# Scaling all three quarters of the gathered rows on ACT in a graph kernel on one Trainium2 core

## The reference

```python
h = jnp.maximum(_layernorm(x, axis=-1), 0.0)
feat_all = jnp.einsum('ni,rhid->rnhd', inputs, conv_weights)      # inputs = h, 8 relations, 4 heads of 64
feat_src_e = feat_all[edge_type, edge_src]                         # a gather per edge, 256 values
el = jnp.sum(feat_src_e * attn_l[edge_type], axis=-1)
er = jnp.sum(feat_dst_e * attn_r[edge_type], axis=-1)
e = jax.nn.leaky_relu(el + er, negative_slope=LEAKY_SLOPE)
m = jax.ops.segment_max(e, edge_dst, num_segments=N_NODES)
ex = jnp.exp(e - m[edge_dst])
alpha = ex / denom[edge_dst]                                       # denom = segment_sum(ex)
h = jax.ops.segment_sum(alpha[..., None] * feat_src_e, edge_dst, num_segments=N_NODES)
...
x = x + h                                                          # then layernorm, relu and the mean network
```

## Time and profile before

| | |
|---|---|
| median of 3 runs | 2599.94 us |
| lowest, highest | 2577.82, 2600.36 us |
| profiled execution: its own time | 2594.63 us |
| profiled execution: span | 2592.7 us |
| mean granted TensorE clock | 0.884 of full |
| gather phase, first to last L1122 | 647.0 to 1450.8 us |

### The profile page before, as it was taken

How to read it: one execution, slowest core, us unless ns; L and a number is a source line. 1 busy time by engine, 2 the same in 40 slices (tenths; PEclk the granted TensorE clock), 3 DMA queues, 4 the chain that set the end, 5 groups by cost and what they waited for, 6 DMA issues and landing times. The chain is left out here.

```text
span 2592.7 us, 29932 instructions
## 1 busy us (share of the span) xinstructions
PE 2173.1 (84%) x9258; PEld 1197.8 (46%) x9259; DVE 1387.6 (54%) x3828; ACT 718.1 (28%) x2133; POOL 584.9 (23%) x549
## 2 busy tenths in 40 slices
PE   2389999995777786778776749999989999999999
PEld 1243334333555464556554424444544444544445
DVE  5779999994456564555565528878821111101001
ACT  0134444442445453445444521010000001000000
POOL 3200000004776665757575100000000000000000
PEclk7589999997776787877777879999989999999999
DMA  5024444445444443535353323222222222233432
GB/s 148 15 97 147 154 148 154 157 154 173 125 126 129 124 140 99 150 103 156 109 152 109 69 89 102 92 82 82 71 83 90 82 86 87 82 115 98 124 98 81
DMA packets 249540, 290.31 MB, mean 112 GB/s; under 512 B 53330, under 2 KB 212247, under 8 KB 249111
## 3 DMA queue, kind: packets, MB, share of 16 engines
q1 hardware_dynamic: 195278, 181.12, 22.8%
q0 software_dynamic: 24192, 67.12, 9.9%
q10 hardware_dynamic: 29896, 39.99, 4.4%
HBM read 201.20 MB, written 86.96 MB: 111 GB/s over the span
## 5 line engine op out<-in xcount | busy, mean ns | idle before, releaser
L1905 PE MATMUL PS<-a_sb,y_sb 128*128 128x512 f16 (+2 forms) x4320 | 874.3, 363 | 43.5 <-DVE y_sb L1981 30.9
L1070 POOL DMA_INDIRECT work<-feat_tab,fidx_i x504 | 543.9, 1079 | 791.3 <-issue 653.1
L1905 PEld LDWEIGHTS PS<-a_sb,y_sb 128*128 128x128 bf16 (+1 forms) x4320 | 407.9, 98 | 509.7 <-issue 69.7
L1275 PE MATMUL PS<-work,stg 128*128 128x260 f32 x1008 | 328.4, 483 | 3.2 <-issue 2.4
L1130 ACT ACTIVATE work<-work 128x64 f32<-128x64 f32 x1344 | 327.3, 332 | 7.5 <-issue 7.1
L233 DVE TENSOR_SCALAR side<-iota_c,col_t 128x512 f16<-128x512 f16 x940 | 329.0, 350 | 0.2
L243 PE MATMUL PS<-side 128*128 128x512 f16 x940 | 254.2, 383 | 20.2 <-DVE side L233 12.4
L1275 PEld LDWEIGHTS PS<-work,stg 128*128 128x128 f32 x1008 | 231.7, 242 | 71.1 <-issue 24.6
L1995 DVE TENSOR_TENSOR mean<-PS,rdeg 128x1024 f32<-128x1024 f32 (+1 forms) x24 | 27.2, 1134 | 416.0 <-PE PS L1905 415.7
L1847 ACT ACTIVATE hT<-mean,bh_c 128x512 f32<-128x512 f32 (+1 forms) x48 | 30.3, 678 | 789.4 <-DVE mean L1999 789.4
L232 DVE TENSOR_SCALAR side<-iota_c,rel 128x128 f16<-128x128 f16 x940 | 236.4, 251 | 0.2 <-PE PS L243 0.2
(11 more groups left out here) (243 smaller groups left out, 1637.0 us busy)
## 6 DMA issues: line engine op xcount, KB each, us to landing
a_sb<-a_tab SPq DMA_DIRECT2D x126, 640.0 KB, 4.3
feat_tab<-stg ACTq DMA_DIRECT2D x120, 260.0 KB, 2.1
a_tab<-side SPq DMA_DIRECT2D x235, 128.0 KB, 1.7
stg<-dst_tab SPq DMA_DIRECT2D x42, 384.0 KB
work<-feat_tab,fidx_i POOLq DMA_INDIRECT x504
h_tab<-outs SPq DMA_DIRECT2D x42, 130.0 KB
h_tab<-outs SPq DMA_DIRECT2D x8, 520.0 KB, 3.2
stg<-h_tab SPq DMA_DIRECT2D x8, 520.0 KB
```

Of the source, the lines that this page charges most:

```text
L1070: pool.indirect_dma_start(out=ring[:, s, 0:FE], out_offset=None, in_=feat_tab[:, :], in_offset=bass.IndirectOffsetOnAxis(ap=idx, axis=0)). ...
L1275: mm = pe.matmul(PS[:, OUTS[j], 0:EXT], onehot[:, t, :], ring[:, j * U + t, 0:EXT], start=(t == 0), stop=(t == U - 1), skip_group_check=True)
L1905: mm = pe.matmul(SUMS(ug, n)[:, f, :], y_sb[l % 2][0:rows_of, kb, s, f * P:(f + 1) * P], a_sb[0:rows_of, load % SLOTS, kb % KB, 0:n], star ...
```

## The change

DVE's `scale` is taken out. ACT's `scale` does a whole quarter at once and is called for all three: quarter 0 right after the weights, then `keep`, then quarter 1, and in the next step quarter 2. The semaphore `s_sd` goes; `quarter_sum` waits for `s_sa` with every quarter, now counted three to a step. At the start of the phase ACT scales quarters 0 and 1 of the first step.

```diff
@@ ACT @@
-                def scale(i, j, q, half):
-                    for u in range(half * QT // 2, (half + 1) * QT // 2):
+                def scale(i, j, q):
+                    for u in range(QT):
                         s = j * U + q * QT + u
                         for h in range(H):
                             a = ring[:, s, h * D:(h + 1) * D]
                             ins = act.activation(a, a, ACT.Copy, scale=ring[:, s, F + h:F + h + 1])
-                    if half:
-                        ins.then_inc(s_sa, 1)
+                    ins.then_inc(s_sa, 1)
...
                 def step(i, j, last=False):
                     nxt = after(i, j, 1)
-                    for half in range(2):
-                        scale(i, j, 2, half)
+                    scale(i, j, 2)
...
                     if not last:
                         act.wait_ge(s_rs, num(i, j, 2, 2))
                         weigh(*nxt)
+                        act.wait_ge(s_ex, num(*nxt, 1, 2))
+                        scale(*nxt, 0)
                     keep(i, j)
                     if not last:
-                        act.wait_ge(s_ex, num(*nxt, 1, 2))
-                        for half in range(2):
-                            scale(*nxt, 1, half)
+                        scale(*nxt, 1)
@@ PE @@
                 def quarter_sum(i, j, q):
                     pe.wait_ge(s_oh, num(i, j, NQT, q + 1))
-                    if q:
-                        pe.wait_ge(s_sa, num(i, j, NQT - 1, q))
-                    else:
-                        pe.wait_ge(s_sd, num(i, j, 1, 1))
+                    pe.wait_ge(s_sa, num(i, j, NQT, q + 1))
@@ DVE @@
-                def scale(i, j):
-                    dve.wait_ge(s_ex, num(i, j, 1, 2))
-                    tiles = slice(j * U, j * U + QT)
-                    rows = ring[:, tiles, 0:F].rearrange("p u (h d) -> p u h d", h=H)
-                    dve.tensor_tensor(rows, rows, ring[:, tiles, F:FE].unsqueeze(3).to_broadcast([P, QT, H, D]), ALU.mult
-                                      ).then_inc(s_sd, 1)
```

More of the change, by code:

```diff
@@ L992, in gnn_kernel @@
         s_fs = [nc.alloc_semaphore(f"feat_stored{i}") for i in range(2)]
-        (s_ix, s_gat, s_sa, s_sd, s_oh, s_db, s_ew, s_oT, s_er, s_sel, s_mk, s_c1, s_v, s_c2, s_r, s_c3, s_cd, s_c4,
+        (s_ix, s_gat, s_sa, s_oh, s_db, s_ew, s_oT, s_er, s_sel, s_mk, s_c1, s_v, s_c2, s_r, s_c3, s_cd, s_c4,
          s_bk, s_ex, s_fx, s_rs, s_grp, s_ev, s_hs, s_kc, s_kp, s_dc) = [sem(a) for a in (
-             "idx_ready", "quarter_summed", "quarters_scaled", "first_quarter_scaled", "onehots_ready", "dst_loaded",
+             "idx_ready", "quarter_summed", "quarters_scaled", "onehots_ready", "dst_loaded",
              "er_window_loaded", "onehotT_ready", "er_ready", "er_selected", "masks_loaded", "scores_ready",
@@ L1196, in begin @@
                     act.wait_ge(s_ex, 2)
-                    for half in range(2):
-                        scale(0, 0, 1, half)
+                    scale(0, 0, 0)
+                    scale(0, 0, 1)
                 walk(act, step, part, begin)
@@ L1476, in step @@
                         bring(i, j)
-                    if not last:
-                        scale(*nxt)
                     if not isinstance(i, int):
@@ L1514, in begin @@
                     onehots(0, 0, 1)
-                    scale(0, 0)
                 walk(dve, step, part, begin)
```

## The result

| | before | after |
|---|---|---|
| median | 2599.06 us (4 runs) | 2634.07 us (4 runs, 2622.76 to 2640.6) |
| ratio, 95% interval | | 1.015, 1.0085 to 1.0214 |
| profiled execution: own time, span | 2594.63, 2592.7 us | 2640.6, 2638.3 us |
| first to last L1122 | 647.0 to 1450.8 | 665.8 to 1493.7 |

The change makes the kernel 35 us slower by the medians; the two profiled executions lie 46 us apart.

A forecast was written before the change was run, and what follows sets the result against it. No engine is full: a path through four engines bounds the gather phase's steps, with ACT on it in the shortest. Terms 35 + 0 + 0 + 0 + 4 + 4 = 43 us on 2599.94 give 2643, rounded to 2640; range 2600 to 2690.

The forecast's parts named there:

- The floor: Gather-phase steps: idle time before L1122 never under about 3.5 us, no interval under 15.5 us.
- Term (1): Sixteen more ACTIVATEs per step on ACT, 3.91 us, paid where idle time before L1122 is short: 35 us, ends 23 and 50.
- The time r: Rest of ACT's idle time before L1122 that can only begin after its last scaling: 3.62 to 5.34 us, taken as 4.45.
- long steps of 21 us should stay: Sign to check after the change: long gather-phase steps, where PE's completions come late, remain at 21 us.
- rival A: Gather phase: hidden after all, a stretched short step gives its time back in the next; 2608 us, chance 0.25.
- Term (5), the parts: Node-phase parts inside the gather phase: ACT scales two quarters before each, 3.9 us more; 4 us together, ends 0 and 10.
- The last step: End of the gather phase: nothing follows that could hide the added scalings, so 3.9 us come in full.
- Term (2): First quarter ready later for PE, as ACT scales it instead of DVE: taken as 0, ends 0 and 14 us.
- term (4): ACT's keep moves behind the first quarter, 3.9 us later: taken as 0.
- Term (3): DVE's TENSOR_TENSOR goes, 52 us of DVE's time: taken as 0, at the other end a gain of 17 us.
- Rival B: PE pauses more between quarters and its granted clock falls under 0.70 in the phase: 2667 to 2680 us, chance 0.15.
- Rival C: POOL's gathers set the pace, so removing DVE's operation beside them gains 29 us: 2571 us, chance 0.1.

The follow-up runs named there:

- x3: Kernel before with 16 extra ACTIVATEs a step on ACT into a scratch tile, ahead of quarter 1: 2629.31 us, ratio 1.0140 to the kernel before.
- x4: Kernel before with 16 extra ACTIVATEs a step on ACT into a scratch tile, behind quarter 2: 2599.61 us, ratio 1.0016 to the kernel before.
- x2: Kernel before, but ACT scales quarters 0 and 1 and DVE quarter 2, so ACT has 32 scalings as before: 2627.00 us, ratio 1.0142.
- x1: Changed kernel measured and profiled again without edit: 2638.05 us, ratio 1.0162 to the kernel before.
- x6: Changed kernel with POOL's second-step gathers waiting for PE's second group of products (the pause): 2509.56 us, ratio 1.0188 to the kernel before.
- x5: Kernel before with POOL's second-step gathers waiting for PE's second group of products (the pause): 2471.11 us, ratio 1.0038 to the kernel before.
- x8: Changed kernel with DVE's TENSOR_TENSOR put back as a product into a scratch tile: 2506.06 us, ratio 1.0171 to the kernel before.
- x10: Kernel before with ACT's one quarter ahead of a part moved inside the part, in five parts: 2570.84 us, ratio 0.9965.
- x9: Changed kernel with ACT's two quarters ahead of a part moved into its waits inside it, in five parts: 2616.28 us, ratio 1.0126 to the kernel before.
- x11: Kernel before, but DVE scales two quarters and ACT only the third: 2571.73 us, ratio 0.9963.
- x7: Kernel before without the scaling of quarter 0, DVE only raising its semaphore: 2448.29 us, ratio 0.9936.
- x12: Kernel before with ACT's one quarter moved inside five parts, the same program as x10 run again: 2465.63 us, ratio 1.0017.

## Why the prediction was right, and where its sum was not

The forecast (2640, slower by 20 to 60 us) held: 2634, and 35 to 46 us. Its mechanism, that work ahead of a quarter is paid, is borne out. The sizes of its terms did less well than its total.

- *The floor* is there, 0.5 us lower than named: no idle time before the mark under 2.95 us for about 3.5, steps of 15.0 for 15.5, sums at 4.3, 8.4 and 12.2 us for 4.3, 8.3 and 12.3. x3 and x4 show that it is work ahead of a quarter, and not ACT's load, that costs. But x2 costs as much without reaching this floor.
- *Term (1)*, 35 us for the 35 intervals, had a range of 23 to 50. The profiles give 12.1 (first pair), 23.9 (x1) and, behind the pause, 14.4 in 27 intervals (x6 against x5). Two steps of it are off. The time r that must follow ACT's last scaling was taken as 3.62 to 5.34 us, and the floor shows 2.95: in the kernel before, ten intervals are under 15.0 us, and they lack 13.6 us of it in all. And "long steps of 21 us should stay": of 11 over 20 us, 6 are left in the first profile, 10 in x1. On the faster chip the other half of the rule, that each short step grows for good, is what failed: in x5, 14 intervals lack 40.1 us of 15.0, and only 14.4 are paid. The rest of the 40.1 had no price, since POOL's twelve gathers paced the mean and a short step only used up a lead. That was the premise of rival A, to which I gave 0.25.
- *Term (5), the parts*, 4 us with an end at 10, can't be settled on the slower chips: 11.9 in the first pair, 1.8 in x1. On the faster chip it is mis-sized, 25.3. The idle time before L1165 that was to hide it, 1.55 to 5.7 us and more, was put down to "remote", and is 2.3 us in all in x5, where no wait is put down to "remote". The steps that used to catch up had gone as well. The last step was to cost 3.9 us; what follows the last mark grew by 2.7, and by 4.9 in x6.
- *Term (2)* at 0 is in doubt: x2, which has the late first and second quarter and not the longer turn, is 31 us slower by the medians, an unknown share of it from its late start. No run asks about *term (4)* alone. *Term (3)* at 0 holds in x8, where the floor sets the pace.
- *The late start*, 18.8 us of the 46, has no term, and isn't the change's. The program up to the first mark is that of the kernel before in x10, and it is there (665.3); so it was in x1, x2, x3 and x9, and not in x4 and x11. How much of the medians' 35 us it makes isn't known.
- *Rival B*, a clock under 0.70, didn't come: 0.75 where it was 0.76. Inside the parts of x6 a lower clock did cost some 6 us more than in x5. *Rival C* was refused on "now it does in one of 42", and this was too much to conclude from one chip: in x5 the score waited for gathers in 26 cases, and x7 collected 13.8 of its 29 us. The 29 were too much because they took 0.70 us a step from one gather, and the mean gather gives 0.46 for all twelve (1.08 us, and 1.04 without the operation). The Trainium skill (SBUF — State Buffer, Who interferes with whom) has DVE and GpSimd share a pair of ports as an exclusive lock. The gathers' means agree with some interference, x6 against x8 too (1.046 and 1.071 us), and no run here shows that the ports are its cause.

That 43 us met 46 is partly luck: 23 too much in (1), 8 too little in (5), 19 from the start, 1 too much at the end. In x1 it was 11, 2 and 4 too much in the same terms, and 18 from the start. Between x5 and x6, free of the late start, the 39.5 us of span came from 8.6 in the inner intervals, 25.3 in the parts, 4.9 at the end and 0.6 at the start (rounded); the 8.6 would be larger without the pause.

## What to carry to other kernels

Where work moves onto the engine with the most idle time, ask what it stands in front of: 3.9 us ahead of a quarter that PE needs cost 1.4%, and the same 3.9 us behind it nothing that could be measured. Don't charge a floor by adding up what the short iterations lack of it: where another engine runs ahead at a steady pace (16.6 us a step here), part of the stretch is free (14.4 of 40.1 us were paid). Look then at the iterations with extra work, which lose the short ones that used to catch up for them. One profile may show a chip's own delays as slack, so don't count idle time with no releaser named as cover. And where a run is altered at one place, as by the pause, compare the stretch behind it.

## What the runs showed of the hardware

The same program, the kernel before, ran in 2576 to 2599 us on some chips and in 2460 to 2462 on two others. On the slower ones every profile has waits put down to "remote", 276 to 397 us in 47 to 77 cases (640 to 1500 us), and on the faster ones none has any. Where such a wait can be followed, it is a completion of PE that reaches the waiting engine late: in the kernel after, ACT's mark at 875.09 (above, "remote") waited for a product that PE's timeline has 2.6 us earlier,

```profile
872.22 0.26 PE L1248 MATMUL PS<-ident,shifted 48*128 48x48 f32 x1 [0.55 <-DVE shifted L1435]
```

and the wait for L1223 at the start came to 31.3 us. On the faster chip the phase takes 692 us in x5 where it took 804. Whether a report is late doesn't hang on the order of the program: the start shows it with and without the change. What delays them, and why on some chips only, stays open.

The same eight fp32 matmuls of 128x512 took 3.70 us at a granted clock of 1.00 (863.7 to 867.5 us of x5) and 6.24 at 0.59 (864.1 to 870.4 us of x6). The wait just before them didn't decide which: they took 6.24 us behind 5.61 us of waiting, 6.77 behind 1.74 in x5, and 5.30 behind 1.16 in x12 (852.7 us).
